# Two operands of a slot product, on VectorE alone and on VectorE and GpSimd

## What is computed

```python
def reference(x, ctx_1024, ...):
    x = x + xattn(_layernorm(x), ctx_1024, ctx_1024, Wq, bq, Wk, bk, Wv, bv, We, be)   # 16 heads
    return x + ffn(_layernorm(x), router_w, router_b, expert_up, expert_down)

def ffn(x, router_w, router_b, expert_up, expert_down):
    probs = softmax(x_flat @ router_w + router_b)
    top_w, top_idx = jax.lax.top_k(probs, 2)
    comb = jnp.sum(top_w[..., None] * one_hot(top_idx, 8), axis=1)
    for e in range(8):
        h = gelu(x_flat @ expert_up[e].T)
        output = output + comb[:, e:e + 1] * (h @ expert_down[e].T)
```

## Time and profile before

| | us |
|---|---|
| runs, median of 3 | 402.63 (402.39 to 403.03) |
| the profiled execution | 401.95 |
| its span, first to last instruction | 399.8 |
| TensorE matmul busy | 366.0 |
| VectorE busy | 242.9 |
| ScalarE busy | 180.3 |
| GpSimd busy | 158.6 |

### The profile page before, as it was taken

How to read it: one execution, slowest core, us unless ns; L and a number is a source line. 1 busy time by engine, 2 the same in 40 slices (tenths; PEclk the granted TensorE clock), 3 DMA queues, 4 the chain that set the end, 5 groups by cost and what they waited for, 6 DMA issues and landing times.

```text
span 399.8 us, 8317 instructions
## 1 busy us (share of the span) xinstructions
PE 366.0 (92%) x2507; PEld 324.2 (81%) x2508; DVE 242.9 (61%) x708; ACT 180.3 (45%) x284; POOL 158.6 (40%) x186
## 2 busy tenths in 40 slices
PE   8989998988998888987999999999999999999990
PEld 8875675667666456987999999999999999999980
DVE  4377496899889967778334557384666266352340
ACT  1354434544433433733533856648384284253230
POOL 2213402402030212115475565564848628626621
PEclk9999999999999999999999999999999999999995
DMA  7920201041040111164232283755729313313312
GB/s 263 351 88 0 107 0 53 2 159 55 0 156 5 53 56 55 55 198 125 55 48 47 40 272 109 185 170 119 237 39 277 54 13 67 53 13 53 54 15 24
DMA packets 26388, 37.23 MB, mean 93 GB/s; under 512 B 4704, under 2 KB 17440, under 8 KB 26368
## 3 DMA queue, kind: packets, MB, share of 16 engines
q1 hardware_dynamic: 19312, 26.98, 20.2%
q0 software_dynamic: 7056, 9.99, 14.4%
HBM read 27.18 MB, written 9.79 MB: 92 GB/s over the span
## 4 chain that ended last, share of the span: by engine, by line
PE 71%; DVE 13%; issue 5%; ACT 3%; DMA 3%; POOL 3%; DVEq 0%; ACTq 0%; POOLq 0%
PE bankC L1257 10%; PE bankC L1259 10%; PE bankC L1258 10%; PE bankD L1622 7%; PE bankD L1624 6%; PE bankD L1623 6%; DVE nmax L797 3%; PE bankC L1456 3%; DMA out<-xn,se 2%; PE bankA L1588 2%; PE bankA L1351 2%; PE bankC L1622 2%; PE bankC L1624 1%; PE bankC L1623 1%; POOL rstd L374 1%
## 5 line engine op out<-in xcount | busy, mean ns | idle before, releaser
L699 ACT ACTIVATE hh<-bankC 128x512 fp32r<-128x512 f32 (+1 forms) x52 | 36.3, 697 | 91.9 <-PE bankC L1259 91.9
L1257 PE MATMUL bankC<-xnT_h,up_w 128*128 128x256 f32 (+1 forms) x240 | 73.7, 307 | 0.5 <-ACT prob L700 0.5
L1258 PE MATMUL bankC<-xnT_l,up_w 128*128 128x256 f32 (+1 forms) x240 | 72.7, 303 | 0.0
L1259 PE MATMUL bankC<-xnT_h,up_w 128*128 128x256 f32 (+1 forms) x240 | 72.7, 303 | 0.0
L1622 PE MATMUL bankD<-dn_w,hh 128*128 x208 | 60.9, 293 | 2.6 <-issue 2.3
L1624 PE MATMUL bankD<-dn_w,hl 128*128 x208 | 58.6, 282 | 0.0
L1623 PE MATMUL bankD<-dn_w,hh 128*128 x208 | 58.5, 281 | 0.0
L450 POOL DMA_INDIRECT xr<-rows,idx_g x35 | 44.0, 1257 | 14.8 <-issue 13.9
L1183 DVE TENSOR_TENSOR hl<-prob,hh 128x512 fp32r<-128x512 f32 (+1 forms) x26 | 21.2, 815 | 43.3 <-ACT prob L700 43.3
L1257 PEld LDWEIGHTS bankC<-xnT_h,up_w 128*128 128x128 f32 x240 | 45.1, 188 | 1.1 <-ACT prob L700 0.7
L1258 PEld LDWEIGHTS bankC<-xnT_l,up_w 128*128 128x128 f32 x240 | 45.2, 188 | 0.0
(11 more groups left out here) (315 smaller groups left out, 866.0 us busy)
## 6 DMA issues: line engine op xcount, KB each, us to landing
xall<-up SPq DMA_DIRECT2D x24, 256.0 KB, 3.9
xall<-down SPq DMA_DIRECT2D x24, 256.0 KB, 5.1
rows<-xr SPq DMA_DIRECT2D x4, 528.0 KB, 3.3
raw<-up SPq DMA_DIRECT2D x4, 512.0 KB, 4.7
raw<-down SPq DMA_DIRECT2D x4, 512.0 KB, 5.4
out<-xall SPq DMA_DIRECT2D x4, 512.0 KB, 3.0
xall<-x SPq DMA_DIRECT2D x1, 1536.0 KB, 8.5
cst<-const SPq DMA_DIRECT2D x1, 640.0 KB, 8.3
```

What stands on the lines that cost most here:

```text
L699: a.activation(hT_h[:, 2 * q:2 * q + 2, 0:n * P], bank, ACT.Gelu)
L1257: mm(out_, left_h, right_h, start=first, stop=False)
L1258: mm(out_, left_h, right_l, start=False, stop=False)
L1259: return mm(out_, left_l, right_h, start=False, stop=last)
```

## The change

The making of `put` goes from VectorE to GpSimd. VectorE's `puts` makes only `hot`; GpSimd has a `puts(b)` of its own, with all eight q. It is called after `value_blocks(2)` (b = 0), after `value_blocks(3)` (b = 1), right after that once more (b = 2), and after the last `halves_rstd2`, ahead of `add_early(0, 0)` (b = 3). The new semaphore `g_put` counts them; TensorE waits for it where it waited for `v_put`, and VectorE waits for the last eight before it writes `lrow` and `key` anew.

```diff
+            def puts(b):
+                pool.wait_ge(v_key, 3 * b + 3)
+                for q in range(8):
+                    pool.wait_ge(p_map, 8 * b + max(q - 3, 0) + 1)
+                    g.tensor_scalar(put[:, q % 4, :], c("iota"), key[:, q:q + 1], val[:, q:q + 1],
+                                    ALU.is_equal, ALU.mult).then_inc(g_put, 1)
             for i in range(1, B):
                 key_blocks(i)
                 halves_rstd2(i - 1)
                 value_blocks(i)
+                if i >= 2:
+                    puts(i - 2)
+            puts(B - 2)
...
+            puts(B - 1)
             pool.wait_ge(d_x1, 16 * B)
             add_early(0, 0)
...
                 dve.wait_ge(v_pos, 4 * b + 4)
+                if b:
+                    dve.wait_ge(g_put, 8 * b)
                 v.scalar_tensor_tensor(out=lrow[:, :], in0=ltile[:, :], scalar=-float(P), in1=rank[:, :],
...
                     v.tensor_scalar(hot[:, q % 4, :], c("iota"), lrow[:, q:q + 1], None, ALU.is_equal)\
                         .then_inc(v_hot, 1)
-                    v.tensor_scalar(put[:, q % 4, :], c("iota"), key[:, q:q + 1], val[:, q:q + 1],
-                                        ALU.is_equal, ALU.mult).then_inc(v_put, 1)
...
                     pe.wait_ge(v_hot, 8 * b + q + 1)
-                    pe.wait_ge(v_put, 8 * b + q + 1)
+                    pe.wait_ge(g_put, 8 * b + q + 1)
```

More of the change, by code:

```diff
@@ L278, in build @@
             sem(n) for n in "g_zero g_kbd g_vbd g_rstd1 g_rstd2 g_rw g_pack v_one v_w01".split())
-        g_gi, g_si, a_be, v_be, g_vb = (
-            sem(n) for n in "g_gi g_si a_be v_be g_vb".split())
+        g_gi, g_si, a_be, v_be, g_vb, g_put = (
+            sem(n) for n in "g_gi g_si a_be v_be g_vb g_put".split())
         p_kv, p_xT, p_q, p_s, p_nmT, p_sT, p_av, p_denT = (
```

## The result

The changed kernel takes 417.05 us (median; 416.10 to 417.56) where the kernel before takes 402.51: a ratio of 1.0353, with a 95% interval of 1.0324 to 1.0382. The prediction said 404.6 us and a range up to 411.5. The sign was the forecast's; the size was seven times too small. The profiled execution took 416.1 us, its span is 414.3.

A forecast was written before the change was run, and what follows sets the result against it. TensorE, busy 92% of the span, was taken to wait at four short places for VectorE's `hot` and `put` pairs or GpSimd's queue. Terms 0.82 + 0.29 + 0.81 = +1.9 us on 402.63 gave 404.6 us, range 401.0 to 411.5.

The forecast's parts named there:

- The price of one `put`: Time X of one 128x128 `put` on GpSimd: 0.55 us predicted, with ends of 0.208 and 0.756.
- The pace formulas: GpSimd's puts start every X - 0.045 (0.505 us); X and 0.25 to the product are added for the last one.
- first two places: Ends of batch 2's and batch 3's columns, where TensorE waits for slot products; predicted +0.41 us each, +0.8 together.
- third place: After the batches: the fifth `put` waits for the ring of four buffers, fourth-last to last on the path; predicted +0.3 us.
- much slower: Rival: X 0.756 or more by a general routine (410.8 us), or puts also waiting out a `hot` (411.7); chance 0.20.
- last place: Batch 3's puts, before the slot table, index copy and three gathers TensorE waits for; predicted +0.8 us.
- VectorE held once for each put: VectorE's `hot` gets through once per GpSimd `put`, about 0.1 us behind its end, taking 0.4 to 0.5 us.
- The rival without a hold: `hot` runs on at 0.20 us; each product is 0.1 earlier, 0.3 us in all; no separate chance given.
- `add_early` behind the puts: At the last place its 1.70 us follow the puts, to 182.06, making index copy and gathers 0.8 us later.
- The ends of batches 2 and 3 by the eighth `put`: There the last four products lose their cover and the eighth `put` counts: +0.41 us, twice.
- Nothing is taken back after 190 us: Behind the last place TensorE is busy almost throughout, so the whole shift reaches the end.
- slower at 0.58: Chance of a slower kernel: the forecast's 0.38 and much slower's 0.20; same 0.20, faster 0.22.

## Why the prediction was wrong, step by step

- **The price of one `put`** was the first step that failed: 0.55 us, between bounds of 0.208 and 0.756; it is 0.788, over the upper one. The choice of the multiply as the nearest row failed. A `put` needs 3.3 ns a column where I took 1.68, and 0.36 us fixed where I took 0.19; of the whole, its two scalars are 0.16. The line itself was off as well: a multiply of 128 columns takes 0.46, not 0.40.
- **The pace formulas held at the first two places.** With 0.788 and a start every 0.777 (0.77 measured between products) they give: fourth and eighth product of the first two places, 98.80 + 5.44 + 0.79 + 0.49 = 105.52 against 102.96, so +2.56 twice; third place, bound by the eighth put as in my "much slower", from `val` on, 142.17 + 5.44 + 0.79 + 0.25 = 148.65 against 146.59, +2.06; last place 176.27 + 5.44 + 0.79 + 1.70 = 184.20 against 181.24, +2.96. The sum is +10.1. With the clock kept whole, 2.55, 2.58, 1.15 and 2.73 were measured, 9.0 in all, and 9.5 for the whole kernel. The third place came cheaper than the formula, since `val` was ready 3.77 us after its start there (142.18 to 145.95) and 4.84 in the kernel before: VectorE turned to its next work (`lg`) 1.70 us ahead of the second place's end there, and 0.40 ahead of it in the kernel before. The last came near its number by another way than mine (see `add_early` below). So of the rivals "much slower" (8.2 at 0.756, with a chance of 0.20) had the right path, the eighth put at every place; its reason, a general routine, no run shows, and its 410.8 us leaves out the clock.
- **The half clock** was missing from the prediction, which asked only when work comes and not how fast TensorE then is: 5.1 us of the 14.5. TensorE stood in short waits between these products already (0.16); the change made them three times as long (0.48).
- **VectorE held once for each put** was wrong: `hot` took 0.30 us (predicted 0.4 to 0.5) and starts 0.2 apart. It moved the forecast little, since GpSimd sets the pace in either case. The rival without a hold said so.
- **`add_early` behind the puts** was wrong as a reason, and right in its number. I said that the slot table does not add, since TensorE has other work between its halves. At 0.788 that work (178.36 to 179.96 before) is far too short to hide 6.4 us of puts, and the table came out with the copy. The cover was worked out for 0.55 and not looked at again for the other prices.
- **The ends of batches 2 and 3 by the eighth `put`**: right, the cover of the last four is gone, and it went for 2.55 and 2.58 with the clock whole, 2.73 and 2.72 in the changed kernel, not 0.41.
- **Nothing is taken back after 190 us**: right. The shift is 13.3 at the gathered tiles and 14.5 at the end.
- **Chances**: slower at 0.58 was on the right side. The range took its upper end from 0.756, the dearest row of the trace, as though a form of operation that the trace lacks could not be dearer.

## What to carry to other kernels

An operation form that an engine does not have in the trace has no bound above in other forms' rows; when the sum swings from -4 to +8 us over the candidates, leave room past the dearest. Work out each cover again at both ends of a range, since "the other work hides it" holds at one price and fails at the next. Where many short waits of TensorE grow, ask what clock it is granted behind them. And give the slower engine a piece that it can finish in its idle time before anybody asks, not a share of a row that is waited for.

## What was not expected of the hardware

- GpSimd's tensor_scalar with a comparison and two per-partition scalars: 0.57, 0.79 and 1.21 us for 64, 128 and 256 columns. The Trainium skill (GPSIMD Engine Reference, section 3.1) gives 1.03 cycles an element for up to two operations, at the 1.2 GHz of its section an estimate of 0.86 ns a column; the measured slope is 3.3 ns, and the measurement decides.
- TensorE, at 2.4 GHz and in the middle of a kernel, was granted 1.2 in or right behind each row of products with waits of 0.48 us between them, in four stretches that end by 196.6 us. With wide products of zeros in these waits it kept 2.4. The falls cost 5.1 of 417 us. But the clock fell as well in an execution in which nothing was changed at that place, so it can't be read off the program alone.
- An unbroken row of GpSimd multiplies of two SBUF operands held one subtraction of VectorE until the row was over (4.50 us for 0.68); GpSimd `put`s beside it did not, and one of them was itself held (1.53 for 0.79).
